# Choosing among seven PSUM banks by due time, and starting the quantised feed-forward's tiles two half steps later

## What is computed

```python
h = relu(x0 @ W0.T) * (x0 @ W1.T) @ Wo.T                     # "tok"
h = ln(h + attention(h, 16 heads, window of +-64))           # layer 0: "qkv", units 0..63, "o" 0..3
h = ln(h + bitlinear(square(relu(bitlinear(h, gate))) * bitlinear(h, up), down))   # "ffn" 0..3
h = ln(h + attention(h, 16 heads, causal))                   # layer 1: "qkv", units 64..127, "o" 4..7
h = ln(ln_affine(h + mixture_of_experts(h, 8 experts, top 2)))   # "gate", "route", "send", then a second block
```

## Time and profile before

| | us |
|---|---|
| median of 3 runs | 1064.77 (1064.33 to 1066.39) |
| profiled execution, device time | 1063.28 |
| its span, first to last instruction | 1061.4 |
| first block, span time | 0 to about 700 |
| PE busy in the span | 871.8 (82%) |
| DVE busy | 547.0 (52%) |
| ACT busy | 418.1 (39%) |
| mean granted PE clock | 0.904 of full |

### The profile page before, as it was taken

One profiled execution on the slowest core, in us unless ns is written; L12 is line 12 of the kernel. 1 busy time (PEld: TensorE's weight loads), 2 busy tenths in 40 slices (PEclk: granted clock), 3 DMA queues, 4 the chain that ended last, 5 costly groups with the idle time before them and its releaser, 6 DMA issues. The chain is left out here.

```text
span 1061.4 us, 14085 instructions
## 1 busy us (share of the span) xinstructions
PE 871.8 (82%) x4842; PEld 546.8 (52%) x4842; DVE 547.0 (52%) x2104; ACT 418.1 (39%) x717; POOL 302.7 (29%) x365
## 2 busy tenths in 40 slices
PE   6697999879778768878989889817999999999940
PEld 3454455535435534434634435315687778777830
DVE  1267434569868669868887868331112102211137
ACT  1315334467467367567646445402210220121003
POOL 5101323413424323312325142434022122112232
PEclk9998999879989889989979979857999999999975
DMA  9893251451450450550565430342151344233242
GB/s 351 148 197 38 25 81 18 46 60 19 43 62 14 48 61 1 62 61 1 62 91 88 49 77 22 100 175 81 40 134 20 120 129 92 59 120 69 26 104 79
DMA packets 57510, 81.48 MB, mean 77 GB/s; under 512 B 6624, under 2 KB 51041, under 8 KB 55008
## 3 DMA queue, kind: packets, MB, share of 16 engines
q1 hardware_dynamic: 49520, 70.48, 33.6%
q0 software_dynamic: 7296, 9.47, 5.4%
q10 hardware_dynamic: 624, 0.63, 0.3%
HBM read 35.37 MB, written 19.68 MB: 52 GB/s over the span
## 5 line engine op out<-in xcount | busy, mean ns | idle before, releaser
L1094 DVE CUSTOM_DVE_ANT_0 junk<-ps,maskb 128x256 bf16<-128x256 f32 (+4 forms) x512 | 206.4, 434 | 104.2 <-PE ps L813 102.4
L639 ACT ACTIVATE probs<-ps 128x512 f32<-128x512 f32 (+1 forms) x304 | 158.2, 551 | 110.0 <-PE ps L836 104.5
L1546 PE MATMUL ps<-dxT,qs 128*128 128x320 f32 x512 | 141.3, 437 | 1.3 <-DVE dxT L1610 1.3
L1558 PE MATMUL ps<-ks,hTe 128*128 128x256 f32 x640 | 139.3, 379 | 0.0
L1580 ACT ACTIVATE hTe<-ps,qs 128x640 f32<-128x640 f32 x64 | 50.8, 794 | 204.6 <-PE ps L1546 204.5
L1558 PEld LDWEIGHTS ps<-ks,hTe 128*128 128x128 f32 x640 | 121.1, 190 | 16.3
L836 PE MATMUL ps<-qs,ks 99*128 99x256 bf16 (+4 forms) x512 | 108.7, 299 | 24.6 <-DVE nmax L1094 9.2
L1502 POOL DMA_INDIRECT mixed_rows<-ysb,ids x40 | 61.7, 1544 | 228.3 <-DVE ysb L1630 225.2
L813 PE MATMUL ps<-ks,qs 96*128 96x256 bf16 (+4 forms) x512 | 108.5, 297 | 22.0 <-DMA ks<-parts 9.0
L1546 PEld LDWEIGHTS ps<-dxT,qs 128*128 128x128 f32 x512 | 98.0, 192 | 42.6 <-DVE dxT L1610 1.9
L554 POOL TENSOR_SCALAR_AFFINE_SELECT probs<-probs 128x256 f32<-128x256 f32 (+1 forms) x64 | 40.1, 627 | 227.7 <-ACT probs L639 227.7
(11 more groups left out here) (179 smaller groups left out, 1198.7 us busy)
## 6 DMA issues: line engine op xcount, KB each, us to landing
qs<-parts SPq DMA_DIRECT2D x96, 128.0 KB, 4.9
ks<-parts SPq DMA_DIRECT2D x96, 128.0 KB, 7.7
qs<-w SPq DMA_DIRECT2D x8, 1024.0 KB
ks<-w SPq DMA_DIRECT2D x8, 1024.0 KB, 4.9
dispatched_rows<-att SPq DMA_DIRECT2D x8, 650.0 KB, 17.1
ks<-dispatched_rows SPq DMA_DIRECT2D x4, 650.0 KB, 7.4
x_sb<-xT SPq DMA_DIRECT2D x8, 256.0 KB, 4.1
mixed_rows<-h SPq DMA_DIRECT2D x4, 512.0 KB, 7.7
```

The lines of the kernel that those rows point to most:

```text
L639: act.activation(probs_of(u)[:, heads[0]:heads[-1] + 1, :], turned_bank((u, half, i))[:, 0:len(heads) * w].rearrange("p (j n) -> p j n", n=w),
L1094: ins = dve.tensor_tensor_reduce(out=junk[:, b - (b > V_BANK), a * (hi - lo):(a + 1) * (hi - lo)], in0=score_bank((u, half, i))[:, a * (hi ...
L1546: ins = mm(bank(2 * (n % 2) + c)[:, 0:HC], w1s[:, e % 2, k, m * P:(m + 1) * P], dxT[:, e % 2, k, c * HC:(c + 1) * HC], start=(k == 0), sto ...
L1558: ins = mm(bank(4 + n % 2)[:, 0:D], hTe[:, e % 2, m, t * P:(t + 1) * P], w2s[:, e % 2, m, :], start=(m == 0), stop=(m == MH - 1))
```

## The change

Three edits.

1. `take` no longer gives out the bank that was taken longest ago. It keeps for each bank the time at which its reading is *due*: (half step, part of the half step, count). A unit's reading is due in its own half step, except for those in `READ_LATER` (the ffn's up products one later, the second half of "tok" and others) and the output turned back. `PARTS` gives the part of the half step. The bank with the earliest due reading is taken.
2. `FQT` 3 becomes 4, `FIRST_TILE` 3 becomes 5, and the ffn has 27 steps for 25. DVE's rounding of the rows stays at c = 1. PE's turn and ACT's copy move one half step later; all work of the four tiles moves two, so the last normalisation stands at c = 26 for 24. `DENSE` is the same, so for ffn 0 to 3 the last two steps now lie at eta 85 and 86, 116 and 117, 148 and 149, 180 and 181, where "o" 1 to 4 start (85, 117, 149, 181).
3. In `hidden_scale` the small operation for the output scale (line 1293 before) goes behind the one that ACT waits for (line 1295 before).

No instruction is added or removed, no operand changes shape, and no DMA is moved in the order of its own queue. Line numbers behind the new function grow by 7.

```diff
@@ -102,10 +102,10 @@
     ("send", 0, 196), ("qkv", 7, 196), ("o", 5, 213), ("gate", 1, 217), ("route", 1, 219), ("send", 1, 228),
     ("o", 6, 245), ("gate", 2, 249), ("route", 2, 251), ("send", 2, 271), ("o", 7, 278), ("gate", 3, 282),
     ("route", 3, 284), ("send", 3, 293),)
-STEPS = {"tok": 12, "qkv": 8, "o": 6, "ffn": 25, "gate": 2, "route": 9, "send": 4, "bias": 2, "wq": 4}
-
-
-FQT, FIRST_TILE, PER_TILE = 3, 3, 4
+STEPS = {"tok": 12, "qkv": 8, "o": 6, "ffn": 27, "gate": 2, "route": 9, "send": 4, "bias": 2, "wq": 4}
+
+
+FQT, FIRST_TILE, PER_TILE = 4, 5, 4
 HIDDEN = 1
 QUANT, TURN, DOWN, STATS, NORM = 4, 6, 7, 8, 9
 
@@ -159,41 +159,48 @@
 HALVES = range(min(SCHED), max(max(SCHED), 2 * UNITS + TO_HEADS) + 1)
 
 V_BANK, BANKS = 5, 8
+PARTS = (1, 1, 2, 0, 1, 3)
 def banks_for(kind, n):
 
     return {"s": (0, 1, 2, 3, 4, 6, 7), "t": (0, 1, 2, 3, 4, 6, 7), "d": (0, 1, 2, 3, 4, 6, 7)}[kind]
 
 
-T_LAST, AT, USES, LAST_USE = {}, {}, [0] * BANKS, [0] * BANKS
-
-
-def take(kind, n, key):
-
-    b = min(banks_for(kind, n), key=lambda i: LAST_USE[i])
+T_LAST, AT, USES, FREE_AT = {}, {}, [0] * BANKS, [(-100, 0)] * BANKS
+READ_LATER = {"tok": {"h": 1}, "ffn": {"u": HIDDEN}, "gate": {"l": 1}, "route": {"c": 1}, "bias": {"o": 0}}
+
+
+def take(kind, n, key, later=0, part=1):
+
+    b = min(banks_for(kind, n), key=lambda i: FREE_AT[i])
     AT[kind, key] = (b, USES[b])
     USES[b] += 1
-    LAST_USE[b] = len(AT)
+    FREE_AT[b] = (n + later, part, len(AT))
+
+
+def dense_take(n, phase, i, key, part):
+
+    take("d", n, (phase, i, key), READ_LATER.get(phase, {}).get(key[0], 0), part)
 
 
 for _n in HALVES:
     if 0 <= _n < 2 * UNITS:
         for _i, _ in enumerate(score_heads(_n // 2, _n % 2)):
-            take("s", _n, (_n // 2, _n % 2, _i))
+            take("s", _n, (_n // 2, _n % 2, _i), 0, PARTS[0])
     for _phase, _i, _c in SCHED.get(_n, ()):
         for _key in early_units(_phase, _c):
-            take("d", _n, (_phase, _i, _key))
+            dense_take(_n, _phase, _i, _key, PARTS[4])
     if (_n - TO_ROWS) % 8 == 0 and 0 <= _n - TO_ROWS < 2 * UNITS:
-        take("t", _n, ("n", (_n - TO_ROWS) // 8))
+        take("t", _n, ("n", (_n - TO_ROWS) // 8), 0, PARTS[1])
     if 0 <= _n - TO_TURNED < 2 * UNITS:
         _u, _h = divmod(_n - TO_TURNED, 2)
         for _i, _ in enumerate(turned_heads(_u, _h)):
             T_LAST[_u] = (_u, _h, _i)
-            take("t", _n, (_u, _h, _i))
+            take("t", _n, (_u, _h, _i), 0, PARTS[2])
     if (_n - TO_BACK) % 8 == 0 and 0 <= _n - TO_BACK < 2 * UNITS:
-        take("s", _n, ("b", (_n - TO_BACK) // 8))
+        take("s", _n, ("b", (_n - TO_BACK) // 8), TO_HEADS - TO_BACK, PARTS[3])
     for _phase, _i, _c in SCHED.get(_n, ()):
         for _key in dense_units(_phase, _c):
-            take("d", _n, (_phase, _i, _key))
+            dense_take(_n, _phase, _i, _key, PARTS[5])
 
 STACKED = 16 * 2 * len(Q_PARTS)
 STACKS = ((), ((0, 0),), ((0, 1), (1, 0)), ((0, 2), (1, 1)), ((1, 2),), ((2, 0), (2, 1)), ((2, 2), (3, 0), (3, 1)),
@@ -1290,10 +1297,10 @@
                                                   ALU.max))
                         linked(2)
                         link(2, dve.reciprocal(q[:, 4, t:t + 1], q[:, 3, t:t + 1]))
-                        link(2, dve.tensor_scalar(q[:, 5, t:t + 1], q[:, 3, t:t + 1], wsc[:, 29:30], None, ALU.mult))
                         linked(2)
                         dve.tensor_scalar(q[:, 4, t:t + 1], q[:, 4, t:t + 1], q[:, 2, t:t + 1], 127.0, ALU.mult,
                                           ALU.mult).then_inc(fh_scaled, 1)
+                        link(2, dve.tensor_scalar(q[:, 5, t:t + 1], q[:, 3, t:t + 1], wsc[:, 29:30], None, ALU.mult))
 
                     def hidden_quant(i, t):
                         dve.wait_ge(fh_raised, NT * i + t + 1)
```

## The result

The changed kernel takes 1040.51 us, median of 4 runs (1037.97 to 1041.36), against 1064.55 for the kernel before: ratio 0.977, 95% interval 0.9746 to 0.9793, 24 us faster. The profiled execution took 1040.43 us with a span of 1038.5.

What follows compares the result with a forecast made beforehand. From 202 to 529 us PE and DVE were taken to wait for each other in turn. Turn -8.5, ffn end +1, banks -5, small operation -0.5 gave -13 us: median 1051.8 us, range 1038 to 1066.

Steps and rivals of the forecast that it cites:

- the largest term: At the four ffn turns, 202 to 529 us: moving turn and first tile later gains 8.5 us, ends 0 and 10.4.
- The turn, one half step later: At ffn 0 to 3: scores fill PE's stall, L888's wait falls from 11.5 to some 7 us; PE's side 6.7 us.
- the loop as a whole: At the four turns PE waits for DVE's rounding, then DVE for PE's scores; middle of 6.7 and 10.4: 8.5 us.
- The tiles themselves carry the same work ... I count 0.: Tiles of ffn 0 to 3, two half steps later: meeting other work spreads DVE's load a little better, priced at 0.
- Banks, 5 us: PE's 14.9 us of waits for L1279, 202 to 529 us: banks by due time gain 5 us, ends 0 and 14.9.
- the third that I took: Share of PE's 14.9 us of bank waits for L1279 counted as time saved: 5 us.
- the reading by which this term is 0: Banks: the skill's rotation taken as already fully done by the order in turn; term 0, sum 5 us smaller.
- The end of the ffn under the next output: At "o" 1 to 4: 9.0 us of DVE work moves under 16.4 us of idle time; 1 us loss, ends 0 and 9.0.
- The loss of 1 us: At "o" 1 to 4: cost of each ffn's last work fitting not exactly beneath DVE's idle time.
- the rival in which it makes the kernel slower: Each ffn's end runs into the next "o" and delays PE: sum +4.3 us, median 1069; chance 0.16.
- The clock, counted at 0 and given a chance of 0.15 as a rival of 12.7 us: Around the four turns: shorter stalls leave PE at the upper clock level, 12.7 us more, median 1039; chance 0.15.
- the argument against it: Against the clock rival: the 1.83 us bank stall ahead of the turn and about 7 of L888's 11.5 us stay.

Runs made afterwards that it cites:

- the whole ffn later: All of each ffn two half steps later, distances inside it kept, banks in turn, against the kernel before: 1049.29 us, ratio 0.9856.
- The filler: 24 needless 128 x 128 bf16 turns on PE ahead of each of four waits for the rounded rows, added to the kernel before: 1058.82 us, 0.9957.

## Why the prediction was right, and where it was not

The direction, the stretch in which the gain lies, the length of the others and the end of the waits for the up product were right. The sum was 13 us and the gain is 24, so the time is inside the range by the range's width, with the largest term credited to the wrong edit. By its own steps:

*The turn, one half step later.* Most of its rows came out: ACT's copy no longer holds the gate and up, DVE's first waits after the turns fell from 10.4 to 3.8 us (under 4 said), and L888's 11.5 us fell further than said, to 4.8 for 6 to 9. But the conclusion from the wait to the time failed. With the turn put back, the wait is 11.7 us and the time the same. Nor was the loop as a whole worth 8.5 us: with both of its waits left as long as before (10.4 and 11.0 us), the whole ffn later already gives 15 of the 20 us, which leaves it about 5. The reading that fits is that PE's stall was a cost because the first gate and up followed it and DVE starved behind both. With the tiles away from the turn and the stall back in full, DVE's waits there are 4.6 us.

*"The tiles themselves carry the same work ... I count 0."* This is the step that was mis-sized. The whole ffn later, with the stall intact, gives 15 us, and the tiles' steps alone, under the new banks and with the turn unmoved, 14 us. I had named the coincidences (the hidden scale with split and heads) and, having no row for them, priced them at nothing. One of their results had rows, which I had counted under the banks: PE's waits for L1279, over all lines, fell from 16.2 to 5.3 us with banks still in turn. Which coincidences make up the rest, and whether the front or the end of the ffn pays, stays open.

*Banks, 5 us.* Alone 11 us, on top of the steps 4 us. The waits named did go, and the third that I took was near for the change as a whole and half of the truth for the rule by itself. The Trainium skill ("Perfetto Trace Analysis", Matmuls) has independent matmul groups rotate through different banks. The order in turn did that already, and this kernel still gained 11 us by choosing the bank otherwise, so the reading by which this term is 0 is refuted here.

*The end of the ffn under the next output.* DVE's waits for the output product fell from 16.4 to 8.9 us (about 9 said). PE's waits for the divided heads did not grow, they fell to the 2.8 us of L876 above, from this row of the kernel before:

```profile
PE ps L869 <- DVE att L1136: 4.9, 4, 2.2
```

The loss of 1 us is not seen, and with the first tile at 6 this hole filled further and the time fell again, so the rival in which it makes the kernel slower was wrong in mechanism up to there.

*The clock, counted at 0 and given a chance of 0.15 as a rival of 12.7 us.* PE's idle time fell by 13 to 18 us, and the rest, 6 to 11 us, is PE's busy time at the higher clock, which the sum had at 0. The rival's time is near, but not by its mechanism. It had the 41 us at the lower level around the turns go, and 34 of them are still there: the argument against it, that the stalls ahead of the turn stay, held. What the rival and the sum both missed is that some 16 us less at the lower level lie elsewhere in the stretch, and that the idle time fell for another reason than the turn. The filler shows that the clock at the four turns of the kernel before was worth 4.6 us by itself. The clock's share of the 24 us is read from busy time and granted clock, not isolated by a run of its own.

## What to carry to other kernels

In a software pipeline of several strictly ordered engines, the longest wait of the busiest engine need not be worth its length: ask who starves behind it, and test by putting it back. Moving a phase by one or two steps against the others, with the spacing of its tiles kept, is a cheap thing to sweep (here 1.8% of the time between the first and the best place, with the new banks), while changing that spacing lost two thirds of the gain or more. Where the readers of buffers are late by different amounts, try giving them out by when their reading is due instead of in turn: here that gave 1.0% alone, and about 0.4% once the phase stood better.

## What the runs showed of the hardware that was not expected

Needless work on PE can pay. 24 turns of 128 x 128 in each of four stalls added 96 instructions to the stretch, lifted its granted clock from 0.90 to 0.93, brought eight matmuls behind three of the stalls from 1.03 to 0.62 us, and saved 4.6 us of 1064. In a kernel whose stretch already had 0.93, the same filler brought that group to 0.62 us at one turn of four and saved nothing.
